# Routed second products of a mixture-of-experts layer from fp16 halves, split between ScalarE and VectorE

## The reference, cut to what matters

```python
xn = layernorm(x)                                   # x: 8 x 1024 tokens of 128 values
# attention part: 32 gathered values per token, weighted and summed to one number s
out_attn = broadcast(s) @ W_out + b_out             # = s * (column sums of W_out) + b_out
# mixture of experts, on the same xn
ffn(x, w1, w2, w3) = (silu(x @ w1.T) * (x @ w3.T)) @ w2.T      # 128 -> 256 -> 128
shared = sum of 2 shared experts, for every token
rw, sel = top_k(xn @ router_w.T + expert_bias, 2);  rw = softmax(rw)
routed = sum over 8 experts of (token's weight for the expert) * ffn(xn, expert)
result = x + out_attn + routed + shared
```

## Time and the profile before

| | us |
|---|---|
| median of 3 runs (lowest, highest) | 414.53 (414.44, 414.63) |
| the profiled execution's own time | 413.85 |
| span of its profile, first to last instruction | 411.9 |
| TensorE busy in the span | 369.1 |
| VectorE busy | 323.5 |
| ScalarE busy | 190.1 |
| GpSimd busy | 226.2 |

### The profile page before, as it was taken

The page is one execution under the profiler, slowest core; times in us unless marked ns, Lnnn a source line. Parts: engine busy times, 40 slices in busy tenths (PEclk is TensorE's granted clock), DMA queues, the critical chain, the costliest instruction groups (busy, mean ns, idle before and its releaser), DMA issues.

```text
span 411.9 us, 12484 instructions
## 1 busy us (share of the span) xinstructions
PE 369.1 (90%) x4333; PEld 318.2 (77%) x4333; DVE 323.5 (79%) x865; ACT 190.1 (46%) x446; POOL 226.2 (55%) x184
## 2 busy tenths in 40 slices
PE   0167798789999999999999999999999999999993
PEld 0065565467677777777779999999999999999993
DVE  5988989987987799999996786866666666666663
ACT  2778729395432466676666444322222222222220
POOL 0434500403877777343301999458886766676766
PEclk9999999899999999999999999999999999999998
DMA  8946530000116399978894455665665545453333
GB/s 293 305 100 104 121 86 0 2 0 16 42 57 131 95 174 186 177 162 167 156 124 96 121 185 158 156 107 66 66 69 65 61 56 62 59 70 30 33 29 32
DMA packets 98870, 41.35 MB, mean 100 GB/s; under 512 B 73600, under 2 KB 92416, under 8 KB 98816
## 3 DMA queue, kind: packets, MB, share of 16 engines
q1 hardware_dynamic: 87120, 31.82, 38.1%
q0 software_dynamic: 11264, 8.69, 15.4%
q10 hardware_dynamic: 432, 0.11, 0.1%
HBM read 10.94 MB, written 12.88 MB: 58 GB/s over the span
## 4 chain that ended last, share of the span: by engine, by line
PE 76%; DVE 12%; ACT 6%; DMA 2%; issue 2%; POOL 1%; POOLq 0%; DVEq 0%; ACTq 0%
PE pY L832 18%; PE pY L665 11%; PE pAB L808 8%; PE pAB L806 8%; PE pAB L807 8%; PE pAB L653 5%; PE pAB L655 5%; PE pAB L654 5%; PE pV L677 4%; ACT units L870 3%; DVE hbuf L1207 2%; ACT wsp L941 2%; PE pV L623 2%; DVE hot L1113 1%; DMA xT<-hot 1%
## 5 line engine op out<-in xcount | busy, mean ns | idle before, releaser
L1065 POOL DMA_INDIRECT out_dram<-xT,rows x64 | 99.2, 1550 | 47.9 <-issue 23.8
L1014 ACT ACTIVATE units<-pAB 128x512 f32<-128x512 f32 x78 | 46.4, 594 | 120.8 <-PE pAB L808 120.8
L1053 POOL DMA_INDIRECT sorted_rows<-rows,slot x64 | 67.4, 1052 | 59.0 <-issue 33.5
L806 PE MATMUL pAB<-rows,wsp 128*128 128x128 f16 x512 | 89.0, 219 | 0.0
L808 PE MATMUL pAB<-rows,wsp 128*128 128x128 f16 x512 | 89.0, 219 | 0.0
L807 PE MATMUL pAB<-rows,wsp 128*128 128x128 f16 x512 | 89.0, 219 | 0.0
L832 PE MATMUL pY<-wsp,hbuf 128*128 (+1 forms) x620 | 86.4, 282 | 0.3 <-issue 0.3
L1496 DVE SCALAR_TENSOR_TENSOR hbuf<-pAB,units 128x512 f32<-128x512 f32 x78 | 53.6, 688 | 37.0 <-PE pAB L808 36.8
L832 PEld LDWEIGHTS pY<-wsp,hbuf 128*128 128x128 f32 x620 | 75.5, 192 | 0.6 <-issue 0.5
L665 PE MATMUL pY<-wsp,hbuf 128*128 128x128 f32 x512 | 70.3, 281 | 0.0
L665 PEld LDWEIGHTS pY<-wsp,hbuf 128*128 128x128 f32 x512 | 64.4, 192 | 4.2
(11 more groups left out here) (165 smaller groups left out, 616.0 us busy)
## 6 DMA issues: line engine op xcount, KB each, us to landing
base<-in_x SPq DMA_DIRECT2D x8, 512.0 KB, 7.6
out_dram<-base SPq DMA_DIRECT2D x16, 256.0 KB, 2.4
wraw<-in_wall SPq DMA_DIRECT2D x10, 256.0 KB, 3.0
rows<-hot SPq DMA_DIRECT2D x8, 256.0 KB, 2.9
proj<-sorted_rows SPq DMA_DIRECT2D x27, 68.5 KB
wsp<-in_wall SPq DMA_DIRECT2D x10, 128.0 KB
sorted_rows<-rows,slot POOLq DMA_INDIRECT x64, 2.4
out_dram<-xT,rows POOLq DMA_INDIRECT x64, 3.4
```

The lines of the kernel that those rows point to most:

```text
L806: pe.matmul(o, hi, x(0), start=True, stop=False)
L1053: pool.indirect_dma_start(sorted_rows, bass.IndirectOffsetOnAxis(ap=slot[:, t:t + 1].bitcast(U32), axis=0), rows[:, t, :], None, bounds_ch ...
L1065: pool.indirect_dma_start(out_rows, bass.IndirectOffsetOnAxis(ap=meta[:, t, DEST - CW:DEST - CW + 1].bitcast(U32), axis=0), yt[:, t], None ...
```

## The change

In the routed stage the second products take fp16 halves. `r_hf` now writes fp32 into a new buffer `h32` (three deep). ScalarE copies it to fp16 (`r_high`, lag 3) and VectorE subtracts that copy to get the low half (`r_low`, lag 4); the halves lie in `h16`, the memory of `hbuf`. A second product becomes three fp16 products (high x high, high x low, low x high), 12 per job, and `r_second` has lag 5.

For main tiles 4 to 59 (`LEAN`), the second expert's sum goes to pV, ScalarE scales it into `yv` (its `y_second`, lag 5), and VectorE adds two tiles at a time (`y_pair`, lag 6). The weights are worked out for eight tiles at a time (`GROUPS`; the first group has four).

The routed second weights are loaded as fp32 in a row as soon as the preparation has freed its memory, ahead of the attention's transposes. In shared units 24 to 31 ScalarE writes their high halves and VectorE their low ones (`second_low`), one expert per unit. ScalarE waits in unit 24 for all eight loads. The factor of the split weights is taken back in the tokens' weights. `add_attention` has one buffer in place of two and does product and addition of a block one after the other. VectorE waits for the last attention sum before the routed stage. Three constants share one buffer with the last raw weight.

```diff
@@ constants
+UNIT_W2 = ROUND * 4 - E
+LATE = TILES - 4
+YV, H32 = 4, 3
+GROUP = 4
+LEAN = [job.main and EXTRA_FROM <= job.t < LATE for job in JOBS]
...
@@ SyncE
+            sp.wait_ge(scratch_free, 1)
+            for e in range(NSH, NE):
+                sp.dma_start(raw_second(e), wall[e, :, W2:WCOL]...).then_inc(w2_ready, 16)
             for m in range(APAIRS):
...
-                if m % 4 == 1:
-                    e = NSH + m // 4
-                    if m == 1:
-                        sp.wait_ge(scratch_free, 1)
-                    sp.dma_start(second[:, :, e, :], wall[e, :, W2:WCOL]...).then_inc(w2_ready, 16)
@@ TensorE
-            FIRST, SECOND = 2, 4
+            FIRST, SECOND = 2, 5
...
-                pe.wait_ge(d_hf, q + 1)
+                pe.wait_ge(d_hi, q + 1)
+                pe.wait_ge(d_lo, q + 1)
...
                 if q >= 2:
                     pe.wait_ge(d_y, q - 1)
+                    if LEAN[q - 2]:
+                        pe.wait_ge(d_yv, JOBS[q - 2].t - EXTRA_FROM + 1)
...
-                        mm = pe.matmul(o, hbuf[:, q % 4, c0:c0 + P], w, start=(h == 0), stop=(h == 1))
+                        pe.matmul(o, h16[:, q % 4, 0, c0:c0 + P], hi, start=(h == 0), stop=False)
+                        pe.matmul(o, h16[:, q % 4, 0, c0:c0 + P], lo, start=False, stop=False)
+                        mm = pe.matmul(o, h16[:, q % 4, 1, c0:c0 + P], hi, start=False, stop=(h == 1))
@@ ScalarE
+                if n >= UNIT_W2:
+                    e = NSH + n - UNIT_W2
+                    if e == NSH:
+                        act.wait_ge(w2_ready, 16 * NE)
+                    else:
+                        act.wait_ge(w2_low, e - NSH)
+                    nc.scalar.activation(whi[:, e, W2:WCOL]..., raw_second(e), ACT.Copy, scale=WS).then_inc(w2_hi, 1)
...
+            def r_high(g, r):
...
+                act.wait_ge(d_hf, q + 1)
+                if q >= 4:
+                    act.wait_ge(d_l2, q - 3)
+                nc.scalar.copy(h16[:, q % 4, 0, 0:job.cols], h32[:, q % H32, 0:job.cols]).then_inc(d_hi, 1)
+            def y_second(g, r):
...
+                nc.scalar.activation(yv[:, t % YV, :], pV[:, q % 2, 0:P], ACT.Copy, scale=share_w[:, t, 1:2]).then_inc(d_yv, 1)
-            pipeline(act, NJOB, UNROLL, NJOB // UNROLL, [(0, r_xt), (2, r_silu)])
+            pipeline(act, NJOB, UNROLL, NJOB // UNROLL, [(0, r_xt), (3, r_high), (2, r_silu), (5, y_second)])
@@ GpSimd, r_send
+                if LEAN[job.place]:
+                    pool.wait_ge(d_sum, (t - EXTRA_FROM) // 2 + 1)
+                else:
+                    pool.wait_ge(d_y, max(job.place, LAST_EXTRA) + 1)
@@ VectorE
+            def second_low(e):
+                dve.wait_ge(w2_hi, e - NSH + 1)
...
+                v.scalar_tensor_tensor(by_half(wlo), raw_second(e), WS, by_half(whi), ALU.mult, ALU.subtract).then_inc(w2_low, 1)
...
+            def r_low(g, r):
...
+                dve.wait_ge(d_hi, q + 1)
+                if q >= 4:
+                    dve.wait_ge(d_l2, q - 3)
+                v.tensor_tensor(h16[:, q % 4, 1, 0:job.cols], h32[:, q % H32, 0:job.cols], h16[:, q % 4, 0, 0:job.cols],
+                                ALU.subtract).then_inc(d_lo, 1)
...
+            def y_pair(g, r):
...
+                dve.wait_ge(d_yv, t - EXTRA_FROM + 1)
+                dve.wait_ge(d_y, q + 1)
+                v.tensor_tensor(yt[:, t - 1:t + 1], yt[:, t - 1:t + 1], yv[:, (t - 1) % YV:(t - 1) % YV + 2], ALU.add).then_inc(d_sum, 1)
-            pipeline(dve, NJOB, UNROLL, NJOB // UNROLL, [(4, side_sums), (4, y_first), (4, y_second), (2, r_hf), (3, side_products),
-                                                         (4, load_tiles), (2, extra_shares)])
+            dve.wait_ge(attn_saved, APAIRS)
+            dve.wait_ge(l2, UNITS)
+            pipeline(dve, NJOB, UNROLL, NJOB // UNROLL, [(4, side_sums), (6, y_pair), (5, y_first), (5, y_second), (4, r_low), (2, r_hf), (3, side_products),
+                                                         (4, load_tiles), (2, extra_shares)])
```

More of the change, by code:

```diff
@@ L75 @@
 GRP = 8
+SPENT = {"before": (0, 128), "low_sel": (128, 256), "ones32": (256, 512)}
 NG = HP // GRP
@@ L138 @@
 WRITE_AT = [min(n for n in range(AHEAD, STEPS) if LAST_OF_TURN[n - AHEAD] >= i) for i in range(NB)]
+GROUPS = [(0, EXTRA_FROM // 2)] + [(n, min(n + GROUP, MAIN_STEPS)) for n in range(EXTRA_FROM // 2, MAIN_STEPS, GROUP)]
+GROUP_OF = [k for k, (lo, hi) in enumerate(GROUPS) for _ in range(lo, hi)]
+LEAN = [job.main and EXTRA_FROM <= job.t < LATE for job in JOBS]
+HALVES = [sum(1 for job in JOBS[:q + 1] if job.experts == 2 and not LEAN[job.place]) for q in range(NJOB)]
 def comes_back(a):
@@ L1015, in r_silu @@
                                      scale=1 / (XS * WS)).then_inc(d_silu, 1)
-            pipeline(act, NJOB, UNROLL, NJOB // UNROLL, [(0, r_xt), (2, r_silu)])
+            def r_high(g, r):
+                q = UNROLL * g + r
+                job = JOBS[q]
+                act.wait_ge(d_hf, q + 1)
[3 more added lines that the diff above has]
+            def y_second(g, r):
+                job = JOBS[UNROLL * g + r]
+                q, t = job.place, job.t
+                if not LEAN[q]:
+                    return
+                act.wait_ge(d_l2, q + 1)
+                act.wait_ge(share_ready, GROUP_OF[job.step] + 1)
+                if t >= EXTRA_FROM + YV:
+                    act.wait_ge(d_sum, (t - EXTRA_FROM - YV) // 2 + 1)
+                nc.scalar.activation(yv[:, t % YV, :], pV[:, q % 2, 0:P], ACT.Copy, scale=share_w[:, t, 1:2]).then_inc(d_yv, 1)
+            pipeline(act, NJOB, UNROLL, NJOB // UNROLL, [(0, r_xt), (3, r_high), (2, r_silu), (5, y_second)])
         @block.gpsimd
@@ L1493, in r_hf @@
                 dve.wait_ge(d_silu, q + 1)
+                if q >= H32:
+                    dve.wait_ge(d_lo, q - H32 + 1)
+                v.scalar_tensor_tensor(h32[:, q % H32, 0:job.cols], pAB[:, 2 * (q % 2) + 1, 0:job.cols], 1 / (XS * WS), silu[:, q % 2, 0:job.cols],
+                                       ALU.mult, ALU.mult).then_inc(d_hf, 1)
+            def r_low(g, r):
+                q = UNROLL * g + r
+                job = JOBS[q]
+                dve.wait_ge(d_hi, q + 1)
                 if q >= 4:
@@ L1511, in side_sums @@
             def side_sums(g, r):
                 job = JOBS[UNROLL * g + r]
-                if job.main and job.turns:
-                    dve.wait_ge(side_parts, job.step + 1)
-                    v.tensor_reduce(share_w[:, 2 * job.step:2 * job.step + 2], side_scr[:, job.step % 2], AX.X, ALU.add).then_inc(share_ready, 1)
+                if job.main and job.turns and job.step in [lo for lo, _ in GROUPS]:
+                    n = GROUP_OF[job.step]
+                    lo, hi = GROUPS[n]
+                    dve.wait_ge(side_parts, n + 1)
+                    v.tensor_reduce(share_w[:, 2 * lo:2 * hi], side_scr[:, n % 2, 0:2 * (hi - lo)], AX.X, ALU.add).then_inc(share_ready, 1)
@@ L1536, in y_first @@
                 if job.main:
-                    dve.wait_ge(share_ready, job.step + 1)
+                    dve.wait_ge(share_ready, GROUP_OF[job.step] + 1)
                     if q == LAST_EXTRA + 1:
```

106 lines of the change are left out of this document (64 added, 42 removed).

## The result

The changed kernel takes 448.3 us (median; 447.93 to 448.73) against 414.49 for the kernel before: a ratio of 1.0816, interval 1.08 to 1.0832. The prediction was 417.0, with a range of 407.5 to 424: the sign was right, the size was missed by 31 us. The profiled execution has a span of 446.1 us, 34.2 more than before.

What follows compares the result with a forecast made beforehand. TensorE, never idle in the routed stage, was taken to set the pace. Lean jobs -10.2, GpSimd's hold on `r_low` +11.9, splitting the weights +0.7 and the end +0.1 sum to +2.5 us: 417.0, range 407.5 to 424.

Steps and rivals of the forecast that it cites:

- Second products: Routed stage, TensorE: twelve fp16 products take 0.67 us in place of 0.95, a main job 2.005.
- The lean loop: Lean jobs: a loop over VectorE and TensorE takes 4.21 us per two jobs, gaining 10.2 us over 56 jobs.
- TensorE idle only before the ones behind a pair: Expected sign in lean jobs: TensorE waits only at second products behind a `y_pair`, released by `r_low`.
- Rival 2: Lean jobs: the loop is shorter than counted and TensorE sets the pace, 5.6 us less, 411.4; chance 0.17.
- What GpSimd does to `r_low`: First routed jobs: GpSimd's attention additions hold `r_low`, two operations per job, 3.0 us a job, +11.9 us.
- rivals 1 and 3: First routed jobs: additions hardly hold `r_low`, 407.3 us, chance 0.13; three GpSimd operations per extra job, up to 424.6, chance 0.13.
- Splitting the second weights: Shared units 24 to 31: ScalarE's wait for the loads delays SiLU and `hf` of unit 25, +0.7 us.
- Jobs that are not lean: Routed stage: two sums in a row on VectorE make 2.29 us per main job, 2.40 per extra one.
- The end: Last jobs: steps of 2.29 us add 1.4, a shorter last slot and earlier last send give back; together +0.1 us.
- The sends: GpSimd's sends of the sums: 1.85 to 1.96 us each against 2.04 available, so no bound.
- Rival 4: A wait on ScalarE for late loads (419.3 us) or in the sends (past 437); chance 0.11.

Runs made afterwards that it cites:

- 14: The kernel before, with the routed weights' addresses counted in bytes, so fewer register operations: 414.13 us, ratio 1.0.
- 1: The changed kernel with the routed weights' addresses counted in bytes, which shortens TensorE's register work: 424.78 us.
- 2: The changed kernel with the high half's address used for the low half too, leaving the second weights' low halves out of the result: 433.34 us.
- 3: The changed kernel with two semaphore waits in place of four ahead of lean jobs' second products: 442.24 us.
- 5: The changed kernel with byte addresses and `r_low` ahead of `y_pair` and the y sums in VectorE's list: 416.28 us.
- 10: The changed kernel with GpSimd's 32 attention operations cut to one column, leaving out most of the attention's share: 444.51 us.
- 7: The changed kernel with a semaphore for each of the eight loads of second weights: 447.91 us.
- 12: The changed kernel with byte addresses and `r_low` ahead of the sums, but no lean jobs: 412.84 us.
- 11: The changed kernel with byte addresses, two waits, `r_low` ahead of sums, a semaphore per load, and for 18 jobs the product in PSUM and earlier `r_low`: 406.64 us.
- 13: The kernel of 11 without lean jobs, both sums on VectorE and each tile sent by itself: 404.05 us.

## Why the prediction missed the size

- **Second products: the step that failed.** "Twelve fp16 products at 0.0557 are 0.67 us in place of 0.95", and with it TensorE's 2.005 per main job and the 4.21 us for two. The slot is 1.06 us (347.22 to 348.28) with 0.21 ahead of it, and a job 2.61. The price came from first products, which have one register instruction to three products; second products have a decoding besides and four waits, and no gap in before shows these, since the fp32 products lay over them (14). What a register instruction costs where nothing covers it was put at nothing instead of being bounded, though the trace of before has the lengths: 0.074 us for an address pair, up to 0.154 with a decoding. Shown by 1 (0.40 of the 0.61 us go), 2, 3 and by 5, which has the 2.01.
- **The lean loop** itself was right where it is the bound: 4.30 measured against 4.21 in 1, two by two, released by `r_low`. In the changed kernel it stands behind TensorE's own 2.61, so of "TensorE idle only before the ones behind a pair" nothing was to be seen. Rival 2 had TensorE set the pace, and it did, but at 2.61 us a job and not at 2.005.
- **What GpSimd does to `r_low`**: right in place, with two of its operations per job in the steady stretch; rivals 1 and 3 fell. That the sum came out (+12.1 for +11.9) is partly luck. From the second products of job 0 to those of job 4 it took 14.65 us (232.56 to 247.21) where 12.0 was forecast, and from there to job 18 37.0 (to 284.22) where 39.2 was: 2.80 per job, not 3.0, until the additions end, then 2.52, not 2.40. Only 4.5 to 5.5 us of the sum are the hold (10).
- **Splitting the second weights**: the mechanism is right, the term too small: +1.9 for +0.7, since the last load released ScalarE 4.0 us after its issue. Of the 1.9 about 1 us is that wait (7), and 0.5 is there ahead of it: SiLU 24 starts at 118.09, before at 117.58, and no run says why.
- **Jobs that are not lean** at 2.29 was worked out for the list with the sums ahead of `r_low`, and no run shows it by itself. With `r_low` first they take 2.07 (12), so the lean half of the change is worth nothing there and costs 2.6 to 3.4 us, most of it in sends at the end (5.6 against 2.9 from the last sum to the last send).
- **The end**: +2.8 for +0.1. The last three steps take 7.05 us (6.9 forecast, before 5.40); the 1.0 taken back for the last send was wrong, it starts 3.1 after the last sum ended (439.23 to 442.36), before 1.9.
- **The sends** were no bound: 1.60 on average (64 of them) and 0.30 between them is 1.90, within 1.85 to 1.96, and at 2.61 per job GpSimd waited for sums. Rival 4 fell in this part. In 11 to 13, with jobs of 2.06, most of the first 45 sends do stand back to back (0.30 apart), 1.93 to 1.96 us each, so there GpSimd has hardly any room left.

The Trainium skill (Perfetto Trace Analysis, section "Sequencer Loop") says that an engine's sequencer reads one instruction at a time, hands engine instructions to a queue and carries out control instructions itself. That would make register instructions time in which no product is handed over; the traces agree (steps of 0.20 where 0.074 and 0.120 us of them stand in a row, 0.056 where only 0.074 do).

## What to carry to other kernels

When a change swaps few long instructions for many short ones, count everything that the engine's queue holds between them, register operations and waits too: what the long ones hid for nothing becomes the pace. A profile that doesn't count such instructions shows them as gaps with the releaser "issue"; asked for by line, it gives their lengths. They can be cheap to shorten, as here by counting addresses in bytes. Put the operation that another engine waits for first in its engine's list before moving other work off that engine.

## What the runs showed of the hardware that was not expected

- A second register instruction behind three fp16 products costs TensorE 0.14 us between the experts (0.200 less 0.056), and four semaphore waits ahead of the second products cost 0.15 in the changed kernel, 0.04 where two of them, long over, are left out (3), and nothing in the median job where the register instructions are short (5).
- `r_low` and GpSimd's addition run side by side at full speed as soon as `r_low` reads one operand from PSUM: 0.68 and 1.27 us, against 0.90 and 1.60 in the steady stretch with both in SBUF.
- Where the build has TensorE load the next words with experts into registers, between the experts of jobs 35 and 60, a lean job takes 4.38 and 3.33 us in place of 2.58; the two loads (L739) last 1.28 and 0.77.
